# Causal attention with softmax denominators partly summed on VectorE, and three reorderings of the same decoder kernel

## The chip, the cores and the metric

One core of a Trainium2 chip runs the whole kernel in one launch. The metric is device time in microseconds (us), the median of three runs.

## What is computed

The reference is one decoder block on x of shape (4, 512, 512), each part followed by a residual and a layer norm. Only the first part bears on the largest edit; the third holds the loops of the other two.

```python
# 1: causal attention, 16 heads of 32 columns
qkv = x @ w_attn + b_attn
att = softmax(where(causal, q @ k.T / sqrt(32), -inf))     # (4, 16, 512, 512)
x = layernorm(x + (att @ v) @ w_proj + b_proj)
# 2: four chosen experts, by token id
x = layernorm(x + chosen(x, token_ids, ctx))
# 3: routed experts (top 2 of 8) and a shared expert behind a sigmoid gate
out = layernorm(x + moe_out(x) + sigmoid(x @ Wsg) * (silu(x @ Sg) * (x @ Su)) @ Sd)
```

## The kernel before, in words

**Three phases** follow each other on the same engines: `attention_phase`, `chosen_phase`, `routed_phase`. Each engine has its own instruction stream, and they meet only at semaphores. Matrix products in reduced form are done as three products of high and low parts, so every tensor that TensorE multiplies is first cast (ScalarE, "hi") and subtracted (VectorE, "lo").

**Attention** has 16 groups (`NG`), each of four heads of one batch entry. A group's work is cut into steps, and `attention_steps` writes one list of steps by hand; every engine walks this same list and does its part of each step, so the list sets the order of every engine's queue. The steps are:
- `Q`, `K`, `V`, `PR`: projections in three parts of four matmuls (L488). After the last part of Q or K, ScalarE casts (L636), VectorE makes the low part (L783), and SP issues the DMAs (L363) that stack high and low parts of each head for the next product; ScalarE issues four of K's itself (L641 to L651).
- `P1` (units u = 0 to 9): scores with queries on partitions (L557), of which VectorE takes the row maximum (L796). There are two PSUM buffers, so P1 of unit n waits until VectorE is through with unit n - 2.
- `M`: the maxima turned (L565) and written as an extra row of the queries by ScalarE (L658).
- `P2`: scores with keys on partitions (L578), exponentials on ScalarE (L668) into `p_f`, causal mask on GpSimd (L430). The units hold key tiles so: u = 0 to 3 key tile 0 of four heads; u = 4 to 7 key tile 1 in columns 0 to 384 and key tile 3 in the last 128; u = 8, 9 key tile 2, two heads each.
- `PV` j (L581 to L597): for key tile j, four heads side by side in the array, `psO` += values times `p_f` and `psN` += ones times `p_f`, each over the queries from tile j on, that is 512, 384, 256 and 128 columns. `psN` is thus the sum of the exponentials, the denominator. The key tiles come in the order 0, 1, 3, 2.
- `NORM`, `YH`: VectorE turns and inverts `psN`, multiplies `psO` (L803 to L813); ScalarE and GpSimd split the result (L675, L435). `NH` does the same for the last group in two halves.
- `XT`, `CW`: transposes of later input and weights (L502, L509), copied by ScalarE (L619, L628) and VectorE (L712, L718). `LN1`, `LN2`, `ST`, `ZB`, `LZ`: layer norm, scatter and bias on VectorE and GpSimd. `RT1` to `RT3`: short dependent chains on VectorE that place tokens.

In slot s of the loop stand the Q and K projections of group s + 2 (`head`), with the first P1 units of group s + 1 between them and M(s) behind the fifth part; then PV of group s - 1, one P1 unit and one P2 unit of the next groups after each key tile; in slots 1, 5 and 9 also one `XT` after each of the first two key tiles (`early`); then the remaining P1 and P2 units with V, PR or XT work spread among them. Slots 4, 8, 12 carry V, slots 5, 9, 13 carry PR. In slot 0 there is no PV. SP also writes zeros to scratch memory (L335), four large DMAs behind K of groups 3 to 7.

`Q`, `K`, `V`, `PR`, `M`, `XT`, `CW` share two PSUM banks in turn, in list order; a step waits until the use before it of its bank is read.

**Routed phase.** At its start PE alternates turns (L1513) with the router's logits (L1531); VectorE reads the logits (L2037) and PE turns them (`logits_turn`, L1539). The shared expert runs in 44 steps n: `shared_up` (24 matmuls, L924), `shared_down` (12, L1570 to L1572). On VectorE each `shared_step` (L1948) begins with `split_up(n + 1)` (L1930), for which PE's `shared_up(n + 1)` waits, then L1941, L1946, L1935. In the second half (n from PART = 22) each step is followed by finished work of the output: `routed_add(t)` (two L2007), `moments(t)` (L2011 to L2015), then GpSimd's power (`power`, L1460), then VectorE's `normalise(t)` (L2019). GpSimd's list for the same step (L1490 to L1496) is: gather rows for t + 2 (two indirect DMAs, L1471, each waiting for a routed_add to free its buffer), then power, then the store of the tile before (L1479). `ADD_AT` says which tiles are added at step n, `FINAL_AT` which is finished: tile t is added at PART + t and finished at PART + 1 + t.

## Time and profile before

| | |
|---|---|
| median of 3 runs (lowest to highest) | 1229.55 us (1229.53 to 1230.07) |
| the profiled execution, its own time | 1227.31 us |
| its span, first to last instruction | 1225.6 us |
| PE (TensorE matmul) busy | 1168.6 us, 95% |
| DVE (VectorE) busy | 688.1 us, 56% |
| ACT (ScalarE) busy | 455.7 us, 37% |
| POOL (GpSimd) busy | 267.5 us, 22% |
| mean granted TensorE clock | 0.986 of full |

PEld is TensorE's weight load, SP is SyncE, and SPq and ACTq are their DMA issues. A row of the timeline gives start, duration, engine, line, operation, output and input, how many instructions are merged, and in brackets how long the engine was idle before and what ended it. Attention runs from 0 to about 430 us of the span, the chosen experts to 566 us, the routed phase to the end, its second half from about 1025 us.

### The profile page before, as it was taken

How to read it: one execution, taken by the hardware profiler on the slowest of the kernel's cores; microseconds unless marked ns; L12 is line 12 of the kernel's file. 1: busy time of each engine (PE TensorE's matmuls, PEld its weight loads, DVE VectorE, ACT ScalarE, POOL GpSimd, SP SyncE). 2: the span in 40 equal slices, each digit the busy share in tenths (PEclk: the TensorE clock that was granted, in tenths of full speed). 3: DMA queues.
4: the chain of work that ended last, by engine and by line, in shares of the span. 5: the costliest groups of instructions: out<-in, count | busy, mean ns of one | idle time of the engine just before them, and what ended most of it. 6: DMA issues, size and time to landing. Idle time of an engine off the chain costs nothing.

```text
span 1225.6 us, 20389 instructions
## 1 busy us (share of the span) xinstructions
PE 1168.6 (95%) x6468; PEld 931.7 (76%) x6468; DVE 688.1 (56%) x1501; ACT 455.7 (37%) x706; POOL 267.5 (22%) x390
## 2 busy tenths in 40 slices
PE   6899999999999789999999999999999999899996
PEld 5665666676675568887788888899999998778885
DVE  5676556666656647765467534434334433666744
ACT  3255334434436223322333324344434433333332
POOL 3122404414415401222002530000000001443302
PEclk8989999999999989999999999999999999999999
DMA  8357774423533332333134683344444522655530
GB/s 247 85 164 213 228 233 117 125 69 88 137 86 112 98 119 96 112 121 121 52 103 134 228 267 105 117 148 162 137 150 149 168 84 86 198 182 169 173 121 35
DMA packets 128207, 169.76 MB, mean 139 GB/s; under 512 B 17504, under 2 KB 70752, under 8 KB 128096
## 3 DMA queue, kind: packets, MB, share of 16 engines
q1 hardware_dynamic: 110704, 129.30, 34.6%
q0 software_dynamic: 9776, 32.51, 7.5%
q10 hardware_dynamic: 7616, 6.57, 2.3%
q8 instruction: 57, 0.93, 0.3%
q14 instruction: 54, 0.44, 0.1%
HBM read 95.98 MB, written 47.19 MB: 117 GB/s over the span
## 4 chain that ended last, share of the span: by engine, by line
PE 46%; DVE 4%; POOL 2%; issue 1%; ACT 1%; ACTq 0%
PE bank L861 19%; PE bank L924 16%; PE bank L1570 3%; PE bank L1571 3%; PE bank L1572 3%; POOL routed_rows_io L1471 2%; PE bank L1600 1%; PE bank L1623 1%; DVE shared_held L1930 1%; DVE routed_h_f L1941 1%; ACT routed_h_hi L1709 0%; DVE routed_h_lo L1946 0%; DVE shared_held L1935 0%; DVE acc L2007 0%; POOL routed_rstd L1460 0%
## 5 line engine op out<-in xcount | busy, mean ns | idle before, releaser
L924 PE MATMUL bank<-store,shared_held 128*128 128x512 f32 (+1 forms) x840 | 187.4, 379 | 3.8 <-DVE shared_held L1930 3.2
L924 PEld LDWEIGHTS bank<-store,shared_held 128*128 128x128 f32 x840 | 150.8, 188 | 36.9 <-DVE shared_held L1930 7.3
L488 PE MATMUL psT<-store 128*128 128x512 f32 x576 | 155.3, 404 | 5.1 <-DVE store L712 3.1
L668 ACT ACTIVATE acc<-psE 128x512 f32<-128x512 f32 x160 | 93.0, 599 | 130.3 <-PE psE L578 90.9
L796 DVE CUSTOM_DVE_ANT_0 psS<-psS,attn_mask 128x512 f32<-128x512 f32 (+3 forms) x256 | 119.8, 514 | 30.7 <-PE psS L557 30.5
L488 PEld LDWEIGHTS psT<-store 128*128 128x128 f32 x576 | 104.5, 192 | 24.2 <-issue 3.7
L1471 POOL DMA_INDIRECT routed_rows_io<-sorted_y,routed_pos x32 | 37.0, 1155 | 375.7 <-DMA sorted_y<-routed_rows_io 313.2
L861 PE MATMUL bank<-shared_held,routed_h_hi 128*128 x624 | 116.4, 328 | 0.3 <-DVE routed_h_lo L1971 0.3
L430 POOL TENSOR_SCALAR_AFFINE_SELECT acc<-acc 128x256 f32<-128x256 f32 (+1 forms) x160 | 56.9, 362 | 226.7 <-ACT acc L668 226.5
L861 PEld LDWEIGHTS bank<-shared_held,routed_h_hi 128*128 128x128 f32 x624 | 100.8, 188 | 0.9 <-issue 0.7
L861 PE MATMUL bank<-store 128*128 x351 | 91.1, 403 | 0.0
L557 PE MATMUL psS<-attn_kS,attn_qS 96*128 96x512 f32 (+3 forms) x256 | 73.0, 348 | 8.0 <-DMA attn_kS<-attn_ch_lo 3.4
L557 PEld LDWEIGHTS psS<-attn_kS,attn_qS 96*128 96x128 f32 x256 | 43.3, 190 | 48.6 <-DVE attn_rowmax L796 20.7
L1702 ACT ACTIVATE routed_h_f<-bank 128x512 f32<-128x512 f32 (+1 forms) x46 | 26.7, 579 | 140.9 <-PE bank L924 137.4
L861 PEld LDWEIGHTS bank<-store 128*128 128x128 f32 x351 | 63.5, 189 | 12.0
L578 PE MATMUL psE<-attn_qS,attn_kS 100*128 100x512 f32 (+3 forms) x256 | 69.4, 336 | 2.9 <-ACT acc L668 1.7
L1570 PE MATMUL bank<-shared_held,routed_h_hi 128*128 128x512 f32 x176 | 69.3, 394 | 0.5 <-DVE routed_h_lo L1946 0.5
L1571 PE MATMUL bank<-shared_held,routed_h_hi 128*128 128x512 f32 x176 | 69.3, 394 | 0.0
L1572 PE MATMUL bank<-shared_held,routed_h_lo 128*128 128x512 f32 x176 | 68.4, 389 | 0.0
L924 PE MATMUL bank<-shared_held 128*128 128x512 f32 x264 | 64.5, 397 | 0.0
L1941 DVE TENSOR_TENSOR routed_h_f<-bank,routed_h_f 128x512 f32<-128x512 f32 (+1 forms) x46 | 30.5, 664 | 59.0 <-ACT routed_h_f L1702 58.9
L861 PE MATMUL bank<-shared_held,routed_h_lo 128*128 x312 | 62.8, 323 | 0.0
(292 smaller groups left out, 2011.7 us busy)
## 6 DMA issues: line engine op xcount, KB each, us to landing
sorted_x<-attn_zero SPq DMA_DIRECT2D x19, 768.0 KB, 6.4
shared_raw<-in_L_ffn_Sg_dram SPq DMA_DIRECT2D x44, 256.0 KB
shared_raw<-in_L_ffn_Su_dram SPq DMA_DIRECT2D x44, 256.0 KB
shared_raw<-in_L_ffn_Sd_dram SPq DMA_DIRECT2D x44, 256.0 KB
routed_rows_io<-sorted_x SPq DMA_DIRECT2D x39, 256.0 KB, 2.8
sorted_y<-routed_rows_io SPq DMA_DIRECT2D x39, 256.0 KB, 2.1
attn_qS<-attn_ch_hi SPq DMA_DIRECT2D x128, 64.0 KB
routed_gu_raw<-in_L_ffn_Wg_dram SPq DMA_DIRECT2D x8, 704.0 KB
```

Of the source, the lines that this page charges most:

```text
L430: pool.affine_select(out=at, in_=at, compare_op=ALU.is_ge, fill=drop, base=0, pattern=[[0, at.shape[1]], [1, P]], channel_multiplier=-1).t ...
L488: last = pe.matmul(out, lhs[a](k), rhs[c](k), start=(s[-1] == 0 and k == 0), stop=(s[-1] == 2 and k == KC - 1))
L557: last = pe.matmul(psS[:, n % 2, c0:c0 + (t + 1) * P], q[0:AUX, i, t * P:(t + 1) * P], k[0:AUX, i, 0:(t + 1) * P], start=True, stop=True)
L578: last = pe.matmul(psE[:, n % 2, c0:c0 + (QT - j) * P], k[0:AUX + 4, i, j * P:(j + 1) * P], q[0:AUX + 4, i, j * P:T], start=True, stop=True)
L668: act.activation(p_f[:, u, :], psE[:, n % 2, :], ACT.Exp, scale=SCALE).then_inc(exp_done, 1)
L796: last = dve.tensor_tensor_reduce(scores, scores, mask[:, (3 - t) * P:T], 1.0, BELOW_ALL, ALU.add, ALU.max, rowmax[:, g % 2, t, i:i + 1])
L861: last = pe.matmul(out, lhs[a](k), rhs[c](k), start=(n == 0), stop=(n == 3 * chunks - 1))
L924: last = pe.matmul(out, w[:, slot, at + k * P:at + (k + 1) * P], x_part(k), start=(g == 0 and k == 0), stop=(g == 2 and k == KC - 1))
L1471: pool.indirect_dma_start(out=got[:, n % 4, :], out_offset=None, in_=sorted_y, in_offset=bass.IndirectOffsetOnAxis(ap=pos[k][:, t:t + 1], ...
L1570: pe.matmul(s_y[i], h[0], w[0], start=(c == 0), stop=False)
L1571: pe.matmul(s_y[i], h[0], w[1], start=False, stop=False)
L1572: last = pe.matmul(s_y[i], h[1], w[0], start=False, stop=(c == CH - 1))
```

## The change

It has four edits.
1. For softmax denominators, the PV step no longer multiplies ones with key tiles 1 (queries of tiles 2 and 3) and 3. A new step `SU` on VectorE adds key tile 1 into key tile 2 (128 x 1024 elements) and then key tile 3 into its second half (128 x 512), and a new PE step `PN` multiplies ones with the sum over the last 256 query columns. Key tiles now come in the order 0, 2, 1, 3; SU stands behind PV of tile 2, PN behind PV of tile 3. ScalarE's exponential of unit 4 waits for all four PV and for SU.
2. Slot 0 has an order of its own: M(0) directly behind the first part of Q(2), RT2 parts 1 and 2 around it, P1(1, 0) and P2(0, 0) only ahead of the last part of K(2).
3. `logits_turn(0)` moves from before `shared_up(1)` to behind its first four matmuls.
4. In the second half, from step PART + 3 on, VectorE does moments, then the adds, then normalise; GpSimd does power, then the gathers, then the store. In step PART + 2, one tile's add stays ahead and the other goes between.

```diff
-    order = (0, 1, 3, 2)
+    order = (0, 2, 1, 3)
...
+        if s == 0:
+            steps += head[:1] + [("RT2", 1), ("M", 0), ("RT2", 2)] + head[1:5] + [p2[0], p1[0], head[5], p2[1], p1[1]]
+            head, p1, p2 = [], p1[2:], p2[2:]
...
-                steps += [("PV", s - 1, j)] + p1[n:n + 1] + p2[n:n + 1] + early[n:n + 1]
+                steps += [("PV", s - 1, j)] + [[], [("SU", s - 1)], [], [("PN", s - 1)]][n] + p1[n:n + 1] + p2[n:n + 1] + early[n:n + 1]
...
-    steps += [("DR",)] + [("PV", NG - 1, j) for j in order] + [("NH", 0), ("CW", 9), ("NH", 1)]
+    steps += [("DR",), ("PV", NG - 1, 0), ("PV", NG - 1, 2), ("SU", NG - 1), ("PV", NG - 1, 1), ("PV", NG - 1, 3), ("PN", NG - 1)] + [("NH", 0), ("CW", 9), ("NH", 1)]
...
+                    if j < 2:
+                        upto = (T, 2 * P)[j]
                         for i in range(4):
                             u, c0 = E_AT[j, i]
+                            last = pe.matmul(psN[i * D:(i + 1) * D, j * P:upto], ones[:], p_f[:, u, c0:c0 + upto - j * P],
+                                             start=(j == 0), stop=False, tile_position=(0, i * D))
+                    last.then_inc(pv_done, 1)
+                elif kind == "PN":
+                    g = s[1]
+                    pe.wait_ge(summed, 2 * (g + 1))
+                    for i in range(4):
+                        u, c0 = E_AT[2, i]
+                        last = pe.matmul(psN[i * D:(i + 1) * D, 2 * P:T], ones[:], p_f[:, u, c0:c0 + 2 * P],
+                                         start=False, stop=True, tile_position=(0, i * D))
                     last.then_inc(pv_done, 1)
...
-                        act.wait_ge(pv_done, QT * (g - 1) + {0: 1, 4: 3, 8: 4}[u])
+                        act.wait_ge(pv_done, PVS * (g - 1) + {0: 1, 4: 4, 8: 5}[u])
+                        if u == 4:
+                            act.wait_ge(summed, 2 * g)
...
+                elif kind == "SU":
+                    g = s[1]
+                    dve.wait_ge(mask_done, UNITS * (g + 1))
+                    dve.wait_ge(pv_done, PVS * g + 2)
+                    own = p_f[:, 8:10, :].rearrange("p a (b n) -> p (a b) n", b=2)
+                    dve.tensor_tensor(own, own, p_f[:, 4:8, P:3 * P], ALU.add).then_inc(summed, 1)
+                    dve.wait_ge(summed, 2 * g + 1)
+                    dve.tensor_tensor(own[:, :, P:2 * P], own[:, :, P:2 * P], p_f[:, 4:8, 3 * P:4 * P], ALU.add).then_inc(summed, 1)
...
             turn(7)
-            logits_turn(0)
-            shared_up(1, lambda g: turn(2 * QT + g) if g < QT else None)
+            def turns_within(g):
+                if g == 0:
+                    logits_turn(0)
+                if g < QT:
+                    turn(2 * QT + g)
+            shared_up(1, turns_within)
...
-                for t in ADD_AT.get(n, []):
+                adds = ADD_AT.get(n, [])
+                ahead = 0 if n > PART + 2 else 1
+                for t in adds[:ahead]:
                     routed_add(t)
                 if n in FINAL_AT:
...
                     moments(t)
-                    normalise(t)
+                for t in adds[ahead:]:
+                    routed_add(t)
+                if n in FINAL_AT:
+                    normalise(FINAL_AT[n])
```

GpSimd's loop is changed in the same way (gathers of `adds[:ahead]`, power, the other gathers, the store).

## Rows read from the trace of the kernel before

**Rows 1.** Busy time by windows, attention: window, PE, PEld, DVE, ACT, POOL, PEclk, DMA.
```profile
100.00:150.00 50.00, 48.77 (x332) 32.53 (x325) 30.53 (x105) 22.71 (x36) 17.16 (x34) 1.00 0.67 204
```
**Rows 2.** Timeline of PE in slot 6: ones times key tile 1, then tile 3.
```profile
193.99 0.83 PE L596 MATMUL psN<-acc,attn_ones 128*32 128x384 f32 x8
194.75 0.50 PE L557 MATMUL psS<-attn_kS,attn_qS 96*128 96x384 f32 x2
...
195.71 0.40 PE L596 MATMUL psN<-acc,attn_ones 128*32 128x128 f32 x8
196.04 0.50 PE L557 MATMUL psS<-attn_kS,attn_qS 96*128 96x384 f32 x2
```
**Rows 3.** Timeline of VectorE: subtractions of 128x1024 and of 128x512 elements in SBUF.
```profile
1049.33 1.22 DVE L1930 TENSOR_TENSOR shared_held<-shared_raw,shared_held 128x1024 fp32r<-128x1024 f32 x1
1050.46 0.68 DVE L1941 TENSOR_TENSOR routed_h_f<-bank,routed_h_f 128x512 f32<-128x512 f32 x1
```
**Rows 4.** Timelines of ACT, DVE and PE in the PV part of slot 5.
```profile
164.97 0.58 ACT L619 CAST store<-psT 128x512 fp32r<-128x512 f32 x1
...
165.58 0.69 DVE L712 TENSOR_TENSOR store<-psT,store 128x512 fp32r<-128x512 f32 x1 [2.62 <-ACT store L619]
...
168.43 0.50 PE L557 MATMUL psS<-attn_kS,attn_qS 96*128 96x384 f32 x2 [0.46 <-DVE attn_rowmax L796]
```
**Rows 5.** Timelines of SP's queue in slots 2 and 3, then of ACT and PE.
```profile
92.30 5.81 SPq L363 DMA_DIRECT2D attn_qS<-attn_ch_hi  x8
...
110.20 7.24 SPq L363 DMA_DIRECT2D attn_qS<-attn_ch_hi  x8
...
125.74 3.69 SPq L335 DMA_DIRECT2D sorted_x<-attn_zero  x4
...
127.21 0.69 ACT L636 ACTIVATE attn_ch_hi<-psT,attn_bqk 128x512 fp32r<-128x512 f32 x1 [1.08 <-DMA attn_kS<-attn_ch_lo]
...
224.25 0.50 PE L557 MATMUL psS<-attn_kS,attn_qS 96*128 96x512 f32 x1 [0.79 <-DMA attn_kS<-attn_ch_lo]
```
**Rows 6.** Timelines of ACT, SP and PE in slot 0 and the head of slot 1.
```profile
52.09 0.69 ACT L636 ACTIVATE attn_ch_hi<-psT,attn_bqk 128x512 fp32r<-128x512 f32 x1 [9.12 <-DMA attn_kS<-attn_ch_lo]
54.26 1.86 ACT L658 ACTIVATE attn_qS<-psT 4x2048 fp32r<-4x2048 f32 x1 [1.48 <-PE psT L565]
...
67.06 2.51 SPq L363 DMA_DIRECT2D attn_kS<-attn_ch_hi  x4
...
71.00 0.50 PE L557 MATMUL psS<-attn_kS,attn_qS 96*128 96x512 f32 x1 [0.20 <-DMA attn_kS<-attn_ch_hi]
```
**Rows 7.** Slot 14: busy time in a window, then a row of VectorE's timeline.
```profile
376.00:388.00 12.00, 10.29 (x84) 7.89 (x80) 11.47 (x38) 6.90 (x13) 7.28 (x14) 0.88 0.45 156
...
375.00 1.88 DVE L847 TENSOR_SCALAR attn_z<-attn_z,attn_mv,attn_rstd 128x512 f32<-128x512 f32 x2
```
**Rows 8.** Timelines of POOL and PE at the end of attention.
```profile
402.44 2.20 POOL L430 TENSOR_SCALAR_AFFINE_SELECT acc<-acc 128x256 f32<-128x256 f32 x6
...
403.98 0.85 PE L596 MATMUL psO<-acc 128*32 128x384 f32 x8 [0.78 <-POOL acc L430]
```
**Rows 9.** Timelines of PE and DVE in the second half.
```profile
1042.07 5.74 PE L924 MATMUL bank<-store,shared_held 128*128 128x512 f32 x24
...
1061.93 5.74 PE L924 MATMUL bank<-store,shared_held 128*128 128x512 f32 x24 [2.85 <-DVE shared_held L1930]
...
1060.14 0.60 DVE L2019 TENSOR_SCALAR acc<-acc,routed_mv,routed_rstd 128x512 f32<-128x512 f32 x1 [2.96 <-POOL routed_rstd L1460]
...
1068.73 0.60 DVE L2019 TENSOR_SCALAR acc<-acc,routed_mv,routed_rstd 128x512 f32<-128x512 f32 x1 [1.74 <-POOL routed_rstd L1460]
```
**Rows 10.** The chain that ended last, later in the second half: start, duration, what.
```profile
1121.84 5.44 PE bank L924 x24
1130.03 5.44 PE bank L924 x24
```
**Rows 11.** Start of the routed phase: PE's timeline, then a window (PE, PEclk, DMA).
```profile
571.44 1.05 PE L1539 MATMUL bank<-routed_gu_raw 18*128 18x9 f32 x8 [1.46 <-DVE routed_gu_raw L2037]
...
572.00:576.00 4.00, 4.00 (x16) 0.60 0.92 338
```

More of the change, by code:

```diff
@@ L75, in attention_steps @@
                 steps += [("M", s)]
-        if not head:
+        if s > NG - 3:
             steps += p1[:2] + [("M", s)]
             p1 = p1[2:]
-        else:
+        elif s:
             p1 = p1[3:]
@@ L132, in attention_phase @@
     UNITS = 10
+    PVS = QT + 1
     STACK = 16 * 24
@@ L2126, in _ @@
                     shared_out(HALF)
-                for t in ADD_AT.get(n, []):
+                adds = ADD_AT.get(n, [])
+                ahead = 0 if n > PART + 2 else 1
+                for t in adds[:ahead]:
                     routed_add(t)
```

26 lines of the change are left out of this document (14 added, 12 removed).

## The prediction

> **What bounds the kernel now.** I read the busy shares first, then PE's busy time by windows, then the chain of waits, then the engines' timelines where the four edits fall. TensorE is the bound nearly everywhere: in a window of attention it is busy 48.77 of 50.00 us while VectorE has 30.53 [rows 1]. So matmul time taken away should come off the end, unless something just behind TensorE takes over. The reader should therefore look for what is second in each slot: in some slots it is SP's queue of DMA issues [rows 5], in others VectorE [rows 4, 7], at the end of attention GpSimd's masks [rows 8]. In the second half of the routed phase VectorE, waiting for GpSimd inside each step, already holds TensorE back [rows 9].
>
> **Edit 1, what it takes from PE.** Ones times key tile 1 takes from 193.99 to 194.75, 0.76 us for 384 columns; key tile 3 takes from 195.71 to 196.04, 0.33 us for 128 columns [rows 2]. Tile 1 keeps 128 columns, so it costs 0.33 as well, and tile 3 goes: 0.43 + 0.33 = 0.76 us less per group. PN is the old tile 2 product, moved. Over 16 groups that would be 12.2 us if nothing else moved.
>
> **Edit 1, what it adds.** No instruction of before does these adds, so I take the nearest: a subtraction of 128x1024 has 1.22 us, and the next one starts 1.13 us after it; one of 128x512 from SBUF and PSUM has 0.68 [rows 3]. SU is then 1.22 + 0.04 + 0.68 = 1.94 us until PN may start and about 1.86 us of VectorE per group, 30 us in all. From below, two instructions overlapped would be 1.13 + 0.60; from above, strided operands could make it 2.2. I take 1.9, as elements and types are those of the row. What counts is what stands behind it: on VectorE the row maxima of P1, and on TensorE, PN and then P1.
>
> *A plain slot* (start T is the first product of PV). PV of tile 0 and the units behind it end at T + 2.5, tile 2 at T + 2.95; SU runs from T + 3.5 (the row maxima before it end then) to T + 5.4. TensorE meanwhile does P1, P2, tile 1, P1, P2 and tile 3 and reaches PN at T + 5.8. No wait. The unit after PN needs the maximum of the unit issued before tile 1, ready at T + 6.1. I take a gain of 0.7 of the 0.76.
>
> *Slots 2, 3, 7 and 11 are not paced by PE.* SP issues without a pause from 92.30 through the set at 110.20 to the zeros at 125.74, and the scores and the cast of the next head start only when its last K part lands: ScalarE has waited 1.08 us at 127.21; in slot 7 TensorE has waited 0.79 us at 224.25 [rows 5]. In slot 11 the same unit starts on landing. A shorter PV there only lengthens the wait. Gain 0 in four slots. Left with the full gain are slots 4, 6, 8, 10, 12 and 13: 6 x 0.7 = **-4.2 us**.
>
> *Slots 1, 5 and 9 carry XT inside PV.* SU stands behind VectorE's part of the first XT in the list. In slot 5 that waits for ScalarE's cast of 164.97, which is behind ScalarE's DMA issues, and runs at 165.58 for 0.6 us [rows 4]. SU can start only at 166.2 and is done at 168.1. TensorE reaches PN at 165.9: a wait of 2.2 us where there was none. The maxima of the next units then come 1.9 us later than before, so the unit that started at 168.43 [rows 4] starts near 170.25: 1.8 us later in spite of the 0.76 saved. In slot 9 ScalarE is earlier and I get 1.6; in slot 1 VectorE is busy without a gap up to the next projection, 1.7 to 1.9. I take 1.8 each: **+5.4 us**.
>
> *Slot 14.* VectorE is busy 11.47 of 12 us [rows 7], with the layer norms (1.88 us from 375.00) ahead of SU. SU runs 376.8 to 378.7, PN waits 0.9 us for it, and the sixth P1 unit starts near 381.15 instead of 379.83: **+1.3 us**. Slot 15's end hangs on GpSimd, which works through bias and masks behind a DMA, so nothing is gained: 0.
>
> *The tail.* The last masks are six units from 402.44, done at 404.64; before, the second product needed only eight units and started at 403.98 [rows 8]. Now tile 2 is second and needs all ten: 404.7. SU then runs to 407.1, PN ends at 407.7; before, the last product ended near 406.8. **+0.9 us**.
>
> **Edit 2.** Its target is SP's queue. The 24 stacking DMAs of group 2 start when Q(2)'s low part is made and end at 67.06 + 2.51 = 69.57; the first unit of group 2 starts at 71.00 after a wait of 0.20 for their landing [rows 6]. Nothing in the new order starts them earlier. On the contrary, M(0)'s ScalarE instruction of 1.86 us now stands ahead of Q(2)'s cast. ScalarE is free at 50.6 and its cast ran at 52.09, once a landing came [rows 6]; now it ends M at 52.5 and casts then: **+0.4 us** for the chain. Bank turns make K(2) wait for Q(2)'s low part, so TensorE stands idle from 49 to 54, but it has about 3 us of slack before 71 to make that up. RT2's chain now lies in VectorE's idle time; RT3 runs earlier too. Bounds: -0.5 if ScalarE's M fits before the landing, +2 if the idle time costs clock. The sum of edits 1 and 2 is -4.2 + 5.4 + 1.3 + 0.9 + 0.4 = **+3.8 us**.
>
> **Edit 3.** PE waited 1.46 us at 571.44 for the logits [rows 11]. Now four matmuls of `shared_up(1)` come first; they need 0.93 us and their weights are there. **-1.0 us.** The work behind it is TensorE's.
>
> **Edit 4.** Undisturbed, a step is 1130.03 - 1121.84 = 8.19 us [rows 10]. From 1042.07 [rows 9] to 1121.84 there are nine steps: 79.77 us against 73.71, so 6.06 us are lost. VectorE's step is 8.58 us, in which it stands 1.74 us before normalise, waiting for GpSimd's power behind two gathers, and 2.96 us in the step with two tiles [rows 9]. With moments first and power ahead of the gathers the wait falls under the adds: 8.58 - 1.74 = 6.9 us, below 8.19. Step PART + 1 is unchanged, so its 0.3 us stays; the step at 1061.93 becomes 1059.35 by the same durations, a rest of about 0.5. What stays is 0.9, so **-5.1 us**. The gathers come 1 us later relative to the adds but are used a whole step later. Bounds: -6.06 and 0.
>
> **The sum.** +3.8 - 1.0 - 5.1 = -2.3 us. The profiled run's own time, 1227.31 (span 1225.6 and 1.7 around it), becomes 1225.0; against the median of 1229.55, which lies 2.2 above that run, it is **1227.2**. That is -0.19%, just inside the 0.2% (2.46 us) that a measurement of this kernel can tell.
>
> **Rival 1, the sums stay hidden.** If VectorE's order costs less than I make it, the attention edit gives its 12.2 us less what SP and GpSimd keep (5 x 0.7 and the tail): -8, with the others -14, 1215; half way, 1221. For it: VectorE has 19 us free in 50 [rows 1]. Against it: SU's place in the list behind XT's part [rows 4]. Chance for something in this direction 0.22, clearly faster.
>
> **Rival 2, slower: the clock falls in the new waits.** In the window 572 to 576 the granted clock is 0.60 of full, part of it at the lower level of 1.2 GHz, after VectorE's wait of 1.46 us and little matmul work before it [rows 11]; in slot 14 it is 0.88 around its waits [rows 7]. The waits I expect before PN in slots 5, 9, 1 and 14, each 0.9 to 2.2 us with short ones behind it, are of that size. At 0.60 over 4 us one such fall costs 1.6 us. With four of them and one after slot 0's idle time it adds 6 to 8 us: 1233 to 1235. It decides from two falls on that cost more than the 2.3 us I have. The Trainium skill's page "TensorE: Matmul & The Clock Gate", section on the clock gate, says that the throttled state is the default and that activity releases it, so idle stretches are paid twice; the window of 572 to 576 agrees, but waits of the same kind elsewhere left the clock at 1.00, such as the 0.78 us at 403.98. Chance 0.2.
>
> **Rival 3, edit 4 does not hold.** If gathered rows come late because GpSimd's gathers now follow power, VectorE waits in the adds instead, and the 5.1 us shrink to 1 or 2: 1231. For it: power itself waits for moments, so a gather can be held by VectorE. Against: buffers are freed a whole step ahead. Chance 0.1. The forecast itself has the other 0.48, from 1225 to 1230.
>
> **How the numbers follow.** Faster by over 0.2% is 1227.1 or less: a little under half of the forecast's own 0.48, rival 1's 0.22: 0.44. Within 0.2%: the rest of the forecast, rival 3 and a little of rival 2, 0.37. Slower than 1232.0: most of rival 2, 0.19. The range runs from 1218, rival 1 with more than half of its gain, to 1233, the beginning of rival 2; that leaves out about 2 in 10. The forecast's own range is 1225 to 1230.
>
> **What would show it.** PE's waits for VectorE before PN: about 2 us in slots 1, 5 and 9, 0.9 in slot 14, none in slots 4, 6, 8, 10, 12, 13. SU's two instructions: 1.2 and 0.7 us. The first unit of group 2 at 71.4. The waits for K's landing in slots 3 and 7 longer by the gain. From end of attention to the chosen phase about 3.8 us later than before. In the second half no wait of VectorE for the power, and `shared_up` every 8.19 us from PART + 4 on. The prediction is wrong if PN waits nowhere, if the clock falls in attention more often than before, or if the second half gives less than 4 us.

## The result, and the profile after

The changed kernel takes 1231.95 us in the median of 20 runs (1227.39 to 1238.14); the kernel before takes 1229.06 in 20 runs on the same chip (1224.00 to 1231.18). The ratio is 1.0032, 95% interval 1.0021 to 1.0043: **3.9 us slower**, outside what I called no change. I had forecast 2.3 us faster. The time lies inside my range of 1218 to 1233; the direction is wrong.

The profiled execution of the changed kernel took 1234.61 us (span 1232.9), so it is one of its slower ones. Its page has these rows of busy time and of clock:

```profile
PE 1166.2 (95%) x6340; PEld 932.5 (76%) x6340; DVE 715.7 (58%) x1533; ACT 456.9 (37%) x706; POOL 275.5 (22%) x390
...
PEclk8899999989999989999999999999999999999999
```

VectorE has 27.6 us more than before (688.1), as the additions were meant to cost. TensorE has only 2.4 us less than before, though 12.2 us of products went. The missing 9.8 us are mostly TensorE doing the same work at half the clock. With `--windows` over every stretch whose granted clock is 0.50, TensorE is busy 38.9 us in such stretches here and 22.0 us in the profile before; half of the 16.9 us between them is 8.5. One long window of attention, first before, then after (columns as in [rows 1]):

```profile
80.00:380.00 300.00, 293.15 (x1953) 197.84 (x1949) 187.56 (x581) 127.41 (x193) 97.14 (x181) 1.00 0.50 144
```

```profile
80.00:380.00 300.00, 285.20 (x1782) 195.44 (x1781) 200.57 (x581) 124.10 (x189) 92.81 (x170) 0.98 0.50 144
```

Before, the granted clock stands at 1.00 for all 300 us. After, TensorE is idle 8 us more and the clock is 0.98. Two of the places, in windows of the changed kernel:

```profile
258.00:267.00 9.00, 7.69 (x74) 3.43 (x72) 5.37 (x13) 4.36 (x7) 0.90 (x3) 1.00 0.75 189
267.00:275.00 8.00, 7.45 (x21) 5.88 (x22) 4.70 (x19) 1.19 (x2) 0.70 (x2) 0.57 0.15 33
...
326.00:329.00 3.00, 1.50 (x6) 1.05 (x6) 0.74 (x2) 1.18 (x2) 2.66 (x3) 1.00 0.01 3
329.00:333.00 4.00, 4.00 (x18) 2.21 (x21) 1.59 (x6) 2.56 (x2) 3.40 (x5) 0.57 0.34 80
```

At 267 and at 329 us the clock falls from 2.4 to 1.2 GHz for most of the window; at 267 the engine had 1.3 us without work just before, at 329 it had 1.5 of 3 us.

**Where the 7.3 us of span went**, slot by slot, by the start of the first product with the probabilities in each. These are differences of two profiled executions, and they hold what varies between executions too: kernels whose first slot is that of before begin slot 1's product anywhere from 72.8 to 75.8 us (74.32 in the profile before), and slot 5 without additions is 31.44 us long in the profile before, as with the chosen groups, but 30.7 to 30.8 in five others. Slot 0: +1.6. Slots 1, 5 and 9, those with the turn of the next input: +1.7, +1.1 and +4.7. Slot 11: +3.3. Slot 14: +1.1. Slots 4 and 8: +0.5 together. The seven slots 2, 3, 6, 7, 10, 12 and 13: -3.8. Slot 15: -0.5. From there to the chosen phase +3.2, and its first microseconds, at the lower clock for longer, +1.1. That makes +14.0 where the routed phase begins. The logits give back 2.5 and the second half 4.5; small differences between them make the rest.

Four of these terms hold the lower clock; the windows of these slots and the timelines of their waits show where. Slot 9 is 32.6 us long in three kernels that have the same additions and the same two waits there and keep the full clock; here, with 6.8 us at 0.50, it is 35.4. Slot 1 has 3.4 us at 0.50. TensorE is idle in it for 1.95 us, hardly more than the 1.73 before, because the new waits take the place of an old one; so its +1.7 is the clock and not the waits. Slot 11 has 3.4 us at 0.50 behind a wait of 2.35 us for K's landing, and the projections of the tail have 3.4.

**Slot 9**, timelines of DVE and PE in the changed kernel. L730 is VectorE's part of the early turn (L712 before), L822 and L824 are the two additions, L814 a row maximum, L612 is PN, L560 a unit of scores:

```profile
263.66 0.69 DVE L730 TENSOR_TENSOR store<-psT,store 128x512 fp32r<-128x512 f32 x1 [1.82 <-ACT store L635]
...
264.26 1.29 DVE L822 TENSOR_TENSOR acc<-acc 128x1024 f32<-128x1024 f32 x1
...
265.59 0.69 DVE L824 TENSOR_TENSOR acc<-acc 128x512 f32<-128x512 f32 x1
...
266.20 0.56 DVE L814 CUSTOM_DVE_ANT_0 psS<-psS,attn_mask 128x384 f32<-128x384 f32 x1
266.34 0.64 PE L612 MATMUL psN<-acc,attn_ones 128*32 128x256 f32 x8 [1.29 <-DVE acc L824]
...
268.45 0.80 PE L560 MATMUL psS<-attn_kS,attn_qS 96*128 96x384 f32 x2 [0.43 <-DVE attn_rowmax L814]
```

This is [rows 4] again: VectorE stands 1.82 us before the turn, waiting for ScalarE's cast, and only then begins the additions. TensorE loses 1.29 us before PN. The units of scores behind it wait for row maxima that stand behind the additions. Over all of attention, PE's waits in the changed kernel (total us, times, longest):

```profile
PE psN L612 <- DVE acc L824: 5.8, 5, 1.3
PE psT L491 <- DVE attn_ch_lo L801: 4.9, 1, 4.9
PE psS L560 <- DMA attn_kS<-attn_ch_lo: 4.1, 3, 2.4
PE psS L560 <- DVE attn_rowmax L814: 3.8, 6, 1.3
PE psE L581 <- ACT acc L686: 3.5, 5, 1.6
```

**Slot 8**, a slot that should have gained, on ACT and PE (L657 ScalarE's share of the stacking, L686 exponentials, L581 the logits they read):

```profile
231.48 3.89 ACTq L657 DMA_DIRECT2D attn_kS<-attn_ch_hi  x4
...
235.47 1.78 ACT L686 ACTIVATE acc<-psE 128x512 f32<-128x512 f32 x3 [4.02 <-PE psN L604]
...
236.12 0.49 PE L581 MATMUL psE<-attn_qS,attn_kS 100*128 100x512 f32 x1 [0.88 <-ACT acc L686]
```

ScalarE is in its own DMA issues until 235.4, so TensorE arrives early and waits 0.88 us. Before, slot 8 had no such wait. The saved 0.76 us turned into it.

**The tail** (L433 masks, L598 products with the values, L848 the first step of the last normalisation, L491 the projection):

```profile
412.14 2.20 POOL L433 TENSOR_SCALAR_AFFINE_SELECT acc<-acc 128x256 f32<-128x256 f32 x6
...
414.39 1.28 PE L598 MATMUL psO<-acc 128*32 128x256 f32 x16 [1.50 <-POOL acc L433]
415.17 1.50 DVE L822 TENSOR_TENSOR acc<-acc 128x1024 f32<-128x1024 f32 x1 [3.41 <-PE psO L598]
...
416.70 0.69 DVE L824 TENSOR_TENSOR acc<-acc 128x512 f32<-128x512 f32 x1
417.45 0.64 PE L612 MATMUL psN<-acc,attn_ones 128*32 128x256 f32 x8 [1.33 <-DVE acc L824]
...
418.15 0.45 DVE L848 STREAM_TRANSPOSE acc<-psN 128x256 f32<-128x256 f32 x1 [0.76 <-PE psN L612]
...
420.73 1.67 PE L491 MATMUL psT<-attn_wp_hi,attn_yT_hi 128*128 128x512 f32 x4 [2.06 <-DVE attn_yT_lo L856]
```

From the start of the last masks to the normalisation it takes 6.0 us; before, it took 4.4 (masks at 402.44 in [rows 8], normalisation at 406.84). The projections behind it then run partly at the lower clock: four matmuls take 1.67 us where four take 1.07 to 1.19 at full clock.

**Logits and second half.** In the changed kernel the logits' turn (L1569) waits 0.53 us instead of 1.46, and the window over it has full clock where [rows 11] has 0.60 (timeline, then window):

```profile
585.44 1.05 PE L1569 MATMUL bank<-routed_gu_raw 18*128 18x9 f32 x8 [0.53 <-DVE routed_gu_raw L2073]
```

```profile
584.00:588.00 4.00, 3.47 (x22) 2.71 (x22) 2.39 (x6) 2.24 (x4) 3.39 (x8) 1.00 1.03 337
```

In the second half (timelines of PE and DVE; L950 is `shared_up`, L2055 VectorE's normalise, L1966 the first split) the wait before normalise is 0.62 us in the step with two tiles and then gone, against 2.96 and 1.74 in [rows 9] (over all thirteen steps 3.2 us are left of 20.7, 1.6 of them in the first):

```profile
1053.91 5.78 PE L950 MATMUL bank<-store,shared_held 128*128 128x512 f32 x24 [0.15 <-DVE shared_held L1966]
1062.44 5.74 PE L950 MATMUL bank<-store,shared_held 128*128 128x512 f32 x24
...
1069.78 0.59 DVE L2055 TENSOR_SCALAR acc<-acc,routed_mv,routed_rstd 128x512 f32<-128x512 f32 x1 [0.62 <-POOL routed_rstd L1486]
...
1071.56 5.74 PE L950 MATMUL bank<-store,shared_held 128*128 128x512 f32 x24 [0.63 <-DVE shared_held L1966]
...
1076.55 0.54 DVE L2055 TENSOR_SCALAR acc<-acc,routed_mv,routed_rstd 128x512 f32<-128x512 f32 x1
```

The `shared_up` of 1042.07 [rows 9] is at 1053.91 now, 11.84 us later; that of 1121.84 [rows 10] is at 1129.17 now, 7.33 later. The second half gained 4.5 us.

### The profile page after: what moved, and what is told of

Read it like the earlier page. It is cut to its first block, busy times and chain, and to the rows that moved or that the text cites. A ratio compares the mean times of both kernels' runs of the same rounds, so it can differ in the third digit from the quotient of the medians.

```text
span 1232.9 us, 20180 instructions
## 1 busy us (share of the span) xinstructions
PE 1166.2 (95%) x6340; PEld 932.5 (76%) x6340; DVE 715.7 (58%) x1533; ACT 456.9 (37%) x706; POOL 275.5 (22%) x390
## 4 chain that ended last, share of the span: by engine, by line
PE 49%; DVE 1%; POOL 1%; ACT 1%; issue 0%; DMA 0%; SPq 0%; ACTq 0%
PE bank L887 19%; PE bank L950 18%; PE bank L1600 3%; PE bank L1601 3%; PE bank L1602 3%; PE bank L1630 1%; PE bank L1653 1%; PE bank L1561 0%; POOL routed_rows_io L1497 0%; DVE shared_held L1966 0%; PE bank L1569 0%; PE bank L1543 0%; DMA shared_raw<-in_L_ffn_Sd_dram 0%; POOL out_dram L1505 0%; DVE routed_h_f L1977 0%
## 5 line engine op out<-in xcount | busy, mean ns | idle before, releaser
L950 PE MATMUL bank<-store,shared_held 128*128 128x512 f32 (+1 forms) x840 | 186.5, 378 | 1.1 <-DVE shared_held L1966 1.1
L950 PEld LDWEIGHTS bank<-store,shared_held 128*128 128x128 f32 x840 | 151.3, 188 | 31.9 <-DVE shared_held L1966 2.7
L491 PE MATMUL psT<-store 128*128 128x512 f32 x576 | 157.9, 409 | 8.3 <-DVE attn_ch_lo L801 4.9
L686 ACT ACTIVATE acc<-psE 128x512 f32<-128x512 f32 x160 | 93.2, 598 | 137.0 <-PE psE L581 120.3
L814 DVE CUSTOM_DVE_ANT_0 psS<-psS,attn_mask 128x512 f32<-128x512 f32 (+3 forms) x256 | 118.9, 515 | 16.3 <-PE psS L560 16.0
L491 PEld LDWEIGHTS psT<-store 128*128 128x128 f32 x576 | 105.9, 195 | 28.5 <-DVE attn_ch_lo L801 5.3
L433 POOL TENSOR_SCALAR_AFFINE_SELECT acc<-acc 128x256 f32<-128x256 f32 (+1 forms) x160 | 60.9, 388 | 231.9 <-ACT acc L686 231.7
L560 PE MATMUL psS<-attn_kS,attn_qS 96*128 96x512 f32 (+3 forms) x256 | 74.5, 354 | 10.0 <-DMA attn_kS<-attn_ch_lo 4.1
L560 PEld LDWEIGHTS psS<-attn_kS,attn_qS 96*128 96x128 f32 x256 | 43.5, 194 | 48.7 <-DVE attn_rowmax L814 22.6
L581 PE MATMUL psE<-attn_qS,attn_kS 100*128 100x512 f32 (+3 forms) x256 | 69.6, 337 | 3.7 <-ACT acc L686 3.5
L1977 DVE TENSOR_TENSOR routed_h_f<-bank,routed_h_f 128x512 f32<-128x512 f32 (+1 forms) x46 | 30.7, 667 | 65.0 <-ACT routed_h_f L1738 64.9
L2143 DVE TENSOR_TENSOR routed_t_h<-bank,routed_t_silu 128x352 f32<-128x352 f32 x39 | 20.4, 522 | 75.2 <-ACT routed_t_silu L1826 75.2
L950 PE MATMUL bank<-shared_held 128*128 128x512 f32 x264 | 63.2, 392 | 0.0
```

The source lines that it names most:

```text
L433: pool.affine_select(out=at, in_=at, compare_op=ALU.is_ge, fill=drop, base=0, pattern=[[0, at.shape[1]], [1, P]], channel_multiplier=-1).t ...
L491: last = pe.matmul(out, lhs[a](k), rhs[c](k), start=(s[-1] == 0 and k == 0), stop=(s[-1] == 2 and k == KC - 1))
L560: last = pe.matmul(psS[:, n % 2, c0:c0 + (t + 1) * P], q[0:AUX, i, t * P:(t + 1) * P], k[0:AUX, i, 0:(t + 1) * P], start=True, stop=True)
L581: last = pe.matmul(psE[:, n % 2, c0:c0 + (QT - j) * P], k[0:AUX + 4, i, j * P:(j + 1) * P], q[0:AUX + 4, i, j * P:T], start=True, stop=True)
L686: act.activation(p_f[:, u, :], psE[:, n % 2, :], ACT.Exp, scale=SCALE).then_inc(exp_done, 1)
L814: last = dve.tensor_tensor_reduce(scores, scores, mask[:, (3 - t) * P:T], 1.0, BELOW_ALL, ALU.add, ALU.max, rowmax[:, g % 2, t, i:i + 1])
```

## The experiments

Fourteen kernels in four groups; each group shared its runs of the kernel before. Besides the time, each run lists the mean granted clock. The level is 1.00 or 0.50 at any moment in these traces, so twice what is missing to 1, times the run's time, is the time spent at the lower level: 40 us for the kernel before (mean of its runs 0.984). What such a microsecond costs depends on whether TensorE has work in it. In the middle of attention it costs nearly half: slot 1 is 22.09 us long with 3.4 us at 0.50 in the kernel with the order alone, and 20.52 without in the kernel with the turns alone. In the profile before, TensorE is busy for only 22.0 of its 35 us. The run lists bear this out: among the 20 runs of the changed kernel the time rises by about 0.6 us for each 0.001 of mean clock that is missing, where half of the lower-level time would give 1.2.

**Edit 1 alone.**
```diff
--- changed
+++ edit 1 alone: first slot, logits_turn and second half as before
```


> Edit 1 by itself on the kernel before (new order of the key tiles, SU and PN; first slot, logits and second half as before). Theory A: the waits for SU before PN, about 1.3 us each in slots 1, 5, 9 and the tail, and the later release of the exponentials' tile take back the 12.2 us of products, and TensorE's clock falls behind such waits besides: 6 to 9 us slower than before, with at least two stretches of granted clock 0.50 between 90 and 380 us, where before has none. Theory B: the waits are as in the prediction and the clock stays up there: +3.4 us. Theory C: this edit is about neutral and the loss is the first slot's: within 1.5 us.


Measured: 1240.52 us against 1228.07, ratio 1.0098 (1.0071 to 1.0124), **+12.0 us**; mean clock 0.977, about 58 us at the lower level. The edit I had at +3.4 costs three times that. Theory A is nearest, and its figure is too small. The interval alone reaches from 8.7 to 15.2 us. The stretches of clock 0.50 that theory A asked for are there, at 171 and at 325 us. Its window from 80 to 380 us shows the clock down as in the changed kernel:

```profile
80.00:380.00 300.00, 284.54 (x1780) 193.94 (x1779) 201.60 (x590) 124.15 (x188) 93.30 (x171) 0.98 0.49 142
```

The sums over all stretches of clock 0.50, first of the kernel before, then of this one (length, then busy time by engine):

```profile
sum 34.98, PE 22.01 PEld 18.04 DVE 17.32 ACT 12.74 POOL 6.54; mean PE 3.67 PEld 3.01 DVE 2.89 ACT 2.12 POOL 1.09
sum 52.13, PE 41.05 PEld 32.60 DVE 23.05 ACT 15.94 POOL 11.66; mean PE 4.10 PEld 3.26 DVE 2.30 ACT 1.59 POOL 1.17
```

TensorE's 19.0 us more of work in them cost 9.5 us. TensorE is idle 9.5 us more as well (66.5 for 57.0), and what remains, 7.6 us less work, is what the removed products gave: together the 11.4 us by which this profile's span is longer.

**Edit 2 alone.**
```diff
+        if s == 0:
+            steps += head[:1] + [("RT2", 1), ("M", 0), ("RT2", 2)] + head[1:5] + ...
-            if m in (6, 9) and s == 0:
-                one += [("RT2", 1 + m // 9)]
```


> Edit 2 by itself on the kernel before. The prediction's term: +0.4 us. Theory A, from the changed kernel's profile, where the first product with the probabilities starts 1.6 us later (75.90 for 74.32): +1 to +2 us, with TensorE idle near 5 us for the low part of Q(2) and with matmuls at the lower clock behind it. Theory C: the first slot also shifts what comes later in attention and carries most of the loss: +4 us or more.


Measured: 1228.71, ratio 1.0010 (0.9999 to 1.0021), +1.2 us, clock 0.984. Theory A's size, but the interval also holds nothing at all. Theory C is out.

**Edits 3 and 4 alone.**
```diff
-            logits_turn(0)
-            shared_up(1, lambda g: turn(2 * QT + g) if g < QT else None)
+            shared_up(1, turns_within)
...
+                for t in adds[:ahead]:
                     routed_add(t)
...
                     moments(t)
-                    normalise(t)
+                for t in adds[ahead:]:
+                    routed_add(t)
+                if n in FINAL_AT:
+                    normalise(FINAL_AT[n])
```


> Edits 3 and 4 on the kernel before, attention untouched. Theory A: both are worth what the changed kernel's profile shows, 2.5 us at the logits and 4.5 in the second half, since they don't depend on attention: -7 us, about 1222. The prediction's own terms give -6.1. Rival: in the changed kernel they were worth as much only because attention had shifted the transfers: -3 or less.


Measured: 1221.85, ratio 0.9948 (0.9932 to 0.9964), **-6.4 us**. The two together stand without edits 1 and 2; the interval holds my -6.1 and theory A's -7.

**The new order alone.**
```diff
-    order = (0, 1, 3, 2)
+    order = (0, 2, 1, 3)
-                                             start=(j == 0), stop=(j == 2), tile_position=(0, i * D))
+                                             start=(j == 0), stop=(j == 3), tile_position=(0, i * D))
-                        act.wait_ge(pv_done, QT * (g - 1) + {0: 1, 4: 3, 8: 4}[u])
+                        act.wait_ge(pv_done, QT * (g - 1) + {0: 1, 4: 4, 8: 4}[u])
```


> Only the order of the key tiles is changed on the kernel before, 0, 2, 1, 3 for 0, 1, 3, 2; the sums stay four products with ones and VectorE adds nothing. The units 4 to 7 of the probabilities can be rewritten only after the fourth product instead of the third. Theory A: this costs ScalarE's exponentials time in slots 4 and 8 and the tail waits for the last masks: +1 to +3 us, and no low clock in slots 5 to 13. Theory B: order is free but for the tail's masks: 0 to +0.7. Theory D: the order by itself makes the whole loss: +6 or more.


Measured: 1227.88, ratio 1.0002 (0.9991 to 1.0013): nothing. Theory B. The later release of the probabilities' tile costs nothing by itself.

So edit 1 is the loss, and not by its order. The next two kernels take it apart into what it removes and what it adds.

**The additions dropped.** This kernel leaves key tiles 1 and 3 out of the last 256 columns of the denominators, so it doesn't compute the reference.
```diff
-                    dve.tensor_tensor(own, own, p_f[:, 4:8, P:3 * P], ALU.add).then_inc(summed, 1)
-                    dve.tensor_tensor(own[:, :, P:2 * P], ..., p_f[:, 4:8, 3 * P:4 * P], ALU.add).then_inc(summed, 1)
-                    pe.wait_ge(summed, 2 * (g + 1))
-                            act.wait_ge(summed, 2 * g)
```


> Edit 1 on the kernel before, without VectorE's two additions and without any wait for them: key tiles 1 and 3 are left out of the last 256 columns of the denominators. It shows what the removed products are worth by themselves. Theory A (products in their slots are worth nearly their length, the additions and the waits for them cost all the rest): 8 us faster than the kernel before (12.2 less what SP's queue and GpSimd keep), PV to PV 0.6 to 0.8 us shorter in nearly every slot, no clock of 0.50 between 90 and 380 us. Theory B (the slots are held by something else than TensorE, so the products were hidden anyway): within 2 us of before.


Measured: 1224.72, ratio 0.9976 (0.9966 to 0.9986), **-3.0 us**; clock 0.982. With the additions free of charge, 12.2 us of products are worth 3 (1.7 to 4.2). The seven plain slots together become 2.5 us shorter than before, slots 4 and 8 none (ScalarE, as in slot 8 above), and slots 1, 5 and 9 0.1 to 0.8 (slot 5's 0.8 is against the long 31.44; against 30.7 it is nothing). Neither theory's figure; B is nearer. Rival 1, which hoped for 8 us from attention, is out even with nothing added.

**The additions beside the old products.** TensorE does all it did and never waits for them.
```diff
 (the new order alone, and)
+ ([("SU", s - 1)] if n == 1 else [])
+                elif kind == "SU":
+                    ...
+                        if u == 4:
+                            act.wait_ge(summed, 2 * g)
```


> The kernel with the new order alone (equal to before in time), to which VectorE's two additions are added; TensorE still does all the old products and never waits for the additions; only the exponentials that rewrite the tiles do. Theory A (the waits before PN with the falling clock are what costs): little, +1 to +3 us over before, from late row maxima in slots 1, 5, 9 and 14. Theory C (the additions cost through VectorE's time and ScalarE's later exponentials, whoever waits for PN): +8 us or more, as with edit 1 or near it.


Measured: 1240.10 (4 runs), ratio 1.0102 (1.0085 to 1.0118), **+12.5 us**; clock 0.980. My theory A falls here: nobody waits in front of PN, as there is none, and the loss is the same. Theory C holds. Timelines of DVE and PE in slot 5 (L715 the turn, L807 and L809 the additions, L799 row maximum, L558 unit of scores):

```profile
167.65 0.69 DVE L715 TENSOR_TENSOR store<-psT,store 128x512 fp32r<-128x512 f32 x1 [1.89 <-ACT store L620]
...
168.26 1.22 DVE L807 TENSOR_TENSOR acc<-acc 128x1024 f32<-128x1024 f32 x1
...
169.51 0.69 DVE L809 TENSOR_TENSOR acc<-acc 128x512 f32<-128x512 f32 x1
...
170.12 0.56 DVE L799 CUSTOM_DVE_ANT_0 psS<-psS,attn_mask 128x384 f32<-128x384 f32 x1
...
171.04 0.50 PE L558 MATMUL psS<-attn_kS,attn_qS 96*128 96x384 f32 x2 [0.99 <-DVE attn_rowmax L799]
...
172.36 0.51 PE L558 MATMUL psS<-attn_kS,attn_qS 96*128 96x384 f32 x2 [0.54 <-DVE attn_rowmax L799]
```

The additions push the row maxima back, and the units of scores wait for those: 0.99 + 0.54 us. The slot is 32.59 us long against 30.72 with the order alone, +1.87, both at full clock; slots 9 and 14 have +1.4 and +1.2. The wait before PN in the changed kernel is the same loss met one instruction earlier. Slot 1 has +1.3, but there TensorE is idle no longer than with the order alone (1.48 us for 1.68), and 6.8 us are at the lower level for 3.4: that loss is the clock's. The four slots add 5.7 us in this pair of profiles. This profile is the fastest of the four runs, with a mean clock of 0.984; its span is 8.1 us longer than the kernel before's, of which 5.3 are idle time of TensorE and 1.6 the lower clock. The mean of the four runs has some 48 us at the lower level, 8 more than before, worth up to 4 us. What is then left of the 12.5 is not traced.

**The early turns one place later.**
```diff
-                steps += [("PV", s - 1, j)] + ... + p2[n:n + 1] + early[n:n + 1]
+                steps += [("PV", s - 1, j)] + ... + p2[n:n + 1] + (early[n - 1:n] if n else [])
```


> Edit 1 on the kernel before, with the two early turns of the next head's input in slots 1, 5 and 9 issued one place later, behind SU in every engine's list. Theory A: SU no longer stands behind VectorE's part of the turn, which waits for ScalarE's cast; the waits of 1.3 us before PN and of 0.7 behind it in these slots go, 1.9 us in each, and low clock behind them too: 5 to 8 us faster than edit 1 alone (1240.5), so about 1234. Theory B: the wait is VectorE's amount of work, not the order; within 2 us of edit 1 alone.


Measured: 1228.51, ratio 1.0007 (0.9996 to 1.0018): +0.9 us over before, **11 us faster than edit 1 alone**, by one place in the list that every engine walks. Theory A's edit and direction, more than its size. Slot 5 here (L821, L823 the additions, L813 row maximum, L729 the turn, L611 PN, L559 scores):

```profile
162.65 1.22 DVE L821 TENSOR_TENSOR acc<-acc 128x1024 f32<-128x1024 f32 x1
...
163.91 0.69 DVE L823 TENSOR_TENSOR acc<-acc 128x512 f32<-128x512 f32 x1
...
164.51 0.56 DVE L813 CUSTOM_DVE_ANT_0 psS<-psS,attn_mask 128x384 f32<-128x384 f32 x1
...
165.24 0.69 DVE L729 TENSOR_TENSOR store<-psT,store 128x512 fp32r<-128x512 f32 x1
...
165.82 0.61 PE L611 MATMUL psN<-acc,attn_ones 128*32 128x256 f32 x8
...
166.37 0.50 PE L559 MATMUL psS<-attn_kS,attn_qS 96*128 96x384 f32 x2
```

The additions are through 1.2 us before PN, the turn no longer waits for its cast, and PE has no wait. Slots 1, 5 and 9 are 20.13, 30.07 and 30.07 us long, all at full clock, against 20.53, 31.44 and 30.73 before and 22.20, 32.58 and 35.38 in the changed kernel. (Beside the other profiles' 30.7 for slot 5, the gain is some 0.65 us in slots 5 and 9 alike.) About 46 us per run are still at the lower level.

**The same move without additions**, as a control.
```diff
-                steps += [("PV", s - 1, j)] + p1[n:n + 1] + p2[n:n + 1] + early[n:n + 1]
+                steps += [("PV", s - 1, j)] + p1[n:n + 1] + p2[n:n + 1] + (early[n - 1:n] if n else [])
```


> The kernel before with the two early turns of slots 1, 5 and 9 one place later and nothing else. Theory D (the gain of 11.5 us is the additions' getting out from behind the turns): without additions there is nothing to free, within 1.5 us of before. Rival: the turns' old place costs by itself, 3 us or more faster than before.


Measured: 1228.22, ratio 1.0002 (0.9988 to 1.0015). Theory D: the turns' place matters only because the additions stand behind them.

**Edit 1 in groups 0, 4 and 8 alone** (slots 1, 5 and 9).
```diff
+ADDED = (0, 4, 8)
+            added = s - 1 in ADDED
+            for n, j in enumerate((0, 2, 1, 3) if added else (0, 1, 3, 2)):
```


> Edit 1 on the kernel before in groups 0, 4 and 8 alone, those whose additions stand behind the turn of the next input (slots 1, 5 and 9). Theory D, formed from the kernels so far: these three slots carry nearly the whole loss of edit 1, 1.9 us each from VectorE's late row maxima (5.7 in all) and as much again because the clock falls behind them in some executions: +8 to +12 us, and the mean granted clock, 0.984 in the kernel before, is at 0.979 or below. Theory A': they cost only what their waits measure, 5.7 us, and the clock is lost elsewhere (slot 11, slot 14, the tail): +5 to +6, clock 0.983 or above.


Measured: 1234.61 (1229.12 to 1239.56), ratio 1.0054 (1.0035 to 1.0073), **+6.6 us**; clock 0.980, about 49 us at the lower level for 39 in the kernel before. The profiled execution is its fastest, 1229.12 at 0.984, with slots 1, 5 and 9 2.0, 1.1 and 1.9 us longer than before. The clock lies nearer theory D's, the total between the two. The wide range is itself the finding: the slowest execution has a mean clock of 0.975. Where it lost it, only a profile of that execution could say. What the profiles at hand do say is that like waits in like places (1.05 to 1.3 us before PN and 0.25 to 0.55 behind it; with additions beside, 0.9 to 1.0 and 0.5 before the units of scores) go with either clock. Slot 5 keeps it here, in the changed kernel and with additions beside, and loses it in edit 1 alone (34.16 us long) and in the change without edit 2 (35.23). Slot 9 loses it in the changed kernel alone, of five. Slot 1 loses it in all five, and also in two of the eleven profiles whose slot 1 has no additions behind a turn.

**Edit 1 in groups 10, 13, 14 and 15 alone.** The same with `ADDED = (10, 13, 14, 15)`.


> Edit 1 on the kernel before in groups 10, 13, 14 and 15 alone (slot 11, the last two slots and the tail). By the slots of the profiles: slot 11 +3.2 (K's stacks land 2 us late), slot 14 +1.1, slot 15 -0.5, the tail +1.6 and some clock. Theory D: +4 to +6 us. If slot 11's late landing is not of this group's own additions (in the kernel with chosen groups it was not late) but of what ran before, slot 11 stays at 17.3 to 18 us and the whole is +1 to +3.


Measured: 1232.71, ratio 1.0036 (1.0023 to 1.0049), +4.4 us; clock 0.980. Slot 11 is 18.15 us long, so the late landing of slot 11 does not come from this group's own additions. Slot 14 is 1.3 us longer; from slot 15's first product to the chosen phase it is 46.4 us against 42.0, with 6.8 us at the lower level at 412.5, behind the waits of the tail. That is more than I gave it.

**A chosen set of groups, on edits 3 and 4.** `ADDED = (1, 2, 5, 6, 9, 11, 12)`.


> Edits 3 and 4, and edit 1 only in the groups whose slots became shorter in the changed kernel and in edit 1 alone (products with the probabilities in slots 2, 3, 6, 7, 10, 12 and 13); the other nine groups and the first slot as before. Theory A: slots add up one by one, -0.65, -0.7, -0.3, -0.2, -0.65, -0.55, -0.53, together 3.6 us below edits 3 and 4 alone (1221.9): 1218. Rival: what one slot gains the next loses to SP's queue or the clock: within 1 us of 1221.9.


Measured: 1219.36, ratio 0.9939 (0.9923 to 0.9955), -7.5 us. Edits 3 and 4 alone had -6.4 (-8.4 to -4.4), and this has -9.4 to -5.5, so a gain of about 1 us is not established. The time lies between theory A's 1218 and the rival's 1220.9 and over. Slots 2 and 3 together even grew in this profile, 17.78 + 18.91 us against 17.62 + 17.96 before, with 1.42 us of waiting for K's landing in slot 3.

**A mix: ten groups, turns behind, edits 3 and 4.** `ADDED = (0, 1, 2, 4, 5, 6, 8, 9, 11, 12)` with the move above.


> Edits 3 and 4, edit 1 in groups 0, 1, 2, 4, 5, 6, 8, 9, 11 and 12, and the two early turns one place later, behind SU, in slots 1, 5 and 9; first slot, slot 11, 14, 15 and tail as before. Theory D: as the kernel with chosen groups (1219.4), less 0.7 us in each of slots 1, 5 and 9: 1217. Rival: SP's queue and the clock take it: 1219 to 1221.


Measured: 1218.79, ratio 0.9931 (0.9918 to 0.9943), **-8.5 us**; clock 0.985. The fastest kernel of the study by its median, though its interval meets that of the chosen groups and that of edits 3 and 4 alone. The time is 1.8 us above theory D's 1217 and just under the rival's range. Slots 1, 5 and 9 are 20.12, 30.07 and 30.09 us long: the three slots that lost now gain 0.4 to 0.65 each.

**The whole change with the turns behind.**
```diff
 (the changed kernel, and)
-                ... + early[n:n + 1]
+                ... + (early[n - 1:n] if n else [])
```


> The whole change with the two early turns one place later, behind SU, and nothing else. Theory D: the place of the turns is the cause of the loss, so it is worth here what it was on edit 1 alone: 11 us less the clock that edit 2 had already given back, 8 to 11 us faster than the changed kernel (1231.95): 1221 to 1224, some 5 us below the kernel before. Rival: with the new first slot the slots are paced otherwise and it gives 3 us or less.


Measured: 1222.51, ratio 0.9962 (0.9949 to 0.9976), **-4.7 us** against before, where the changed kernel has +3.9: 8.6 us by the ratios, 9.4 by the medians. Theory D.

**The change without edit 2.**
```diff
-        if s == 0:
-            steps += head[:1] + [("RT2", 1), ("M", 0), ("RT2", 2)] + ...
```


> The changed kernel with the first slot of before (edits 1, 3 and 4). If the parts add up, it lies at 12.0 - 6.4 = 5.6 us over before, 1.7 over the changed kernel or, by the first slot's own +1.2, 1.2 below it. If the new first slot gives back a part of edit 1's loss, it lies 3 us or more above the changed kernel, +7 over before, with more time at the lower clock; if the difference is the spread of edit 1's clock, it lies between +2.5 and +5.6.


Measured: 1231.86 (1229.71 to 1238.71), ratio 1.0039 (1.0024 to 1.0053), +4.8 us; clock 0.977. Inside the last of the three ranges. The new first slot neither costs nor gives back anything that can be told inside the whole change, and the sum of parts (+12.0 - 6.4 = +5.6) agrees with this kernel.

## Why the prediction was wrong

**The step that failed** is edit 1: +1.2 in the plain slots and in slots 1, 5 and 9, +3.4 with slot 14 and the tail; measured +12.0 (8.7 to 15.2). The larger part of what was missing is the term that the sum put at nothing: TensorE's clock, which falls behind the new waits. Point by point:

- *Slots 1, 5 and 9, +1.8 each:* mechanism, place and size were right in slots 5 and 9, where the clock stayed up: 32.5 to 32.6 us against 30.7. The additions stood behind the turn as foreseen. The wait before PN is 1.3 us rather than 2.2, with 0.4 to 0.55 before the units behind it. In slot 1 of the changed kernel the total of +1.7 is luck: the waits replaced an older one, and the lower clock cost what they did not (in edit 1 alone the slot has both, +3.2).
- *The clock, left out of the sum and given to rival 2 with 0.2:* this is the term that decided. Edit 1 alone spends about 58 us per run at the lower level against 40. If TensorE is at work in all of the difference, that is 9 of the 12 us, and its profile has 9.5 of 11.4; by the rise of time with clock among its six runs (0.9 us for 0.001) it is 6 to 7. The changed kernel has about 49 us at that level, worth 2 to 4.5 us. The price of one fall was right: 1.6 us in [rows 11] and rival 2, 1.6 us in slot 1. I had set it aside because other waits had left the clock up. What I took from that, that falls are the exception, was the error: behind the same wait the clock falls in some kernels' profiles and not in others, so the price belongs in the sum, weighted. Rival 2 named the waits before PN and slot 0's idle time; the changed kernel's profile has the falls behind PN in slots 1 and 9, and two that it did not name, behind K's landing in slot 11 and in the tail's projections. The Trainium skill's page "TensorE: Matmul & The Clock Gate", section on the clock gate, says that the throttled state is the default and that activity releases it. This case's traces agree: edit 1 alone has 9.5 us more of idle time and loses as much again to the clock.
- *Plain slots, -0.7 in six and 0 in slots 2, 3, 7 and 11:* the total, -3.3 for -4.2 without slot 11, is near by luck. My six slots (4, 6, 8, 10, 12, 13) gave -1.4; slots 2, 3 and 7, which I had at 0, gave -1.9 in the changed kernel (slots 2 and 3 gave nothing in the chosen groups). Slots 4 and 8, which I counted at -0.7 each, gave nothing. ScalarE's DMA issues hold the exponentials there, and I had looked at SP's queue alone.
- *Slot 11, 0:* +3.2 to +4.6 in three of the profiles, by a landing 1.1 to 2.1 us later than elsewhere (below) and by the lower clock behind the wait for it. Not foreseen.
- *Slot 14, +1.3:* measured +1.1. *The tail, +0.9:* +1.6 to the normalisation. GpSimd's masks were right (PE waits 1.50 us), but the addition begins only when tile 2's product is done and takes 1.50 us there, not 1.22; and +1.6 more from there to the chosen phase, about what the projections lose at the lower clock.
- *Edit 2, +0.4:* +1.2 alone (-0.1 to +2.6). ScalarE was not free at 50.6: its own issues lasted to 51.8, so M and the cast behind it ended 1.7 us later than before. The first unit of group 2 started at 72.66, where I had 71.4 and before had 71.00. But shifts of this size (slot 1's product 1.3 us later with the turns alone, 0.5 earlier with additions dropped) come without edit 2 as well, so how much of it is edit 2's stays open.
- *Edit 3, -1.0:* -2.5 in the changed kernel's profile. The wait shrank by the 0.93 us worked out; the rest is the clock that no longer falls there (0.60 to 1.00 in the window). With the old place it falls there in four of ten profiles, the one before among them, with the new place in none of six.
- *Edit 4, -5.1:* -4.5. The nine steps from 1053.91 to 1129.17 take 75.26 us where nine undisturbed ones would take 73.71, so 1.55 us of the 6.06 are left, and I had 0.9. Most of it is in the first two, of 8.53 and 9.12 us, where VectorE's splitting still holds `shared_up` (0.15 and 0.63 us above). Rival 3 is out. Edits 3 and 4 together, forecast -6.1, measured -6.4: in the profile edit 3 gave 1.5 us more and edit 4 0.6 us less than their terms, so the sum is closer than they are.
- *Rival 1* is out: adds_dropped shows that even additions that cost nothing leave only 3 us of gain.

With the changed kernel's lower-level time priced at half, 4.5 us, the sum of -2.3 would have become +2.2, the right sign; with the 2 us that its runs' slope gives, about zero. What stays open: how often the clock falls behind a given wait, which the traces show only one execution at a time, and what makes slot 11's landing late.

## What to carry to other kernels

Work moved from a bound engine to an idle one is placed in that engine's list; what stands in front of it there (here a cast that ScalarE delivers late) prices it more than its own length. One place in the list was worth 11 us of 12. Give every new wait of TensorE two prices, the wait and the lower clock behind it, and put the second into the sum, weighted by how often such waits had it in the traces, rather than into a rival. When a slot of one profile is compared with a slot of another, look first at the clock in both, and at the same slot in kernels where nothing was changed. And where a slot is freed on one engine, look at every queue that runs in it, ScalarE's DMA issues as well as SP's.

## What the runs showed of the hardware that was not expected

**The clock's variation.** The same program spends different times at the lower level: edit 1 in three groups ran from 1229.12 us at a mean granted clock of 0.984 to 1239.56 at 0.975, while the mix kernel, with no wait of that kind, stayed within 0.984 and 0.986 over its five runs.

**A late landing, with an instruction fetch near it.** In slot 11 of three kernels (changed, edit 1 alone, turns behind) PE waited 2.2 to 2.4 us for K's stacks, and went on 16.4 to 16.7 us after the slot's first product; in the other profiles it went on after 14.6 to 15.3. In all three the clock fell behind this wait, and the rest of the slot took 1.4 to 2.6 us longer than in the profiles without a fall there. In edit 1 alone, the unit that waited and, by the DMA view of the window 318 to 319, what moved while the stacks were under way (timeline, then DMA queues):

```profile
324.95 0.80 PE L559 MATMUL psS<-attn_kS,attn_qS 96*128 96x512 f32 x1 [2.19 <-DMA attn_kS<-attn_ch_lo]
```

```profile
q0 software_dynamic: 89, 0.36, 93.2%
q8 instruction: 1, 0.02, 6.0%
```

GpSimd's load of the next input has 93% of the DMA engines in that microsecond, and a fetch of 16 KB of instructions falls into it. In these three kernels the fetch came 9.2 to 9.7 us after the slot's start, in the others by 7.2 us, from 15.7 us on or not at all, and only these three had the late landing in that slot. But landings as late came elsewhere without a fetch at that place: PE went on after 16.5 us in slot 7 with additions beside (fetch at 13.9 us) and after 16.4 us in slot 3 with turns behind (fetch at 13.7 us, no load by GpSimd in the slot), while slot 3 of edit 1 alone, with its fetch at 13.6 us, had no wait. No kernel moved the fetch alone. So the fetch may play a part in slot 11; that it is the cause is not shown, and it can't be the only one.
